# Projections as three one-pass float32r products, and attention masks read as int32 (one core)

## The reference, cut to what matters

```python
q = x @ Wq;  k = ctx @ Wk;  v = ctx @ Wv + bv      # float32, per layer
scores = where(mask == 0, -10000, q.k / 4)         # layer 0: int32 mask [8, 512, 512]
scores = where(causal, scores, -inf)               # layer 1: causal, no mask input
x = softmax(scores) @ v @ Wo + bo + x              # then normalisation and FFN
```

## Time and profile before

| | |
|---|---|
| median of 3 runs | 1360.01 us (1357.59 to 1364.4) |
| the profiled execution | 1357.38 us |
| its span | 1355.6 us |
| PE busy | 1256.7 us (93%) |
| DVE, ACT, POOL busy | 1001.9, 867.9, 512.4 us |
| mean DMA rate | 126 GB/s |

### The profile page before, as it was taken

One profiled execution on the slowest core, in us unless ns is written; L12 is line 12 of the kernel. 1 busy time (PEld: TensorE's weight loads), 2 busy tenths in 40 slices (PEclk: granted clock), 3 DMA queues, 4 the chain that ended last, 5 costly groups with the idle time before them and its releaser, 6 DMA issues. The chain is left out here.

```text
span 1355.6 us, 21435 instructions
## 1 busy us (share of the span) xinstructions
PE 1256.7 (93%) x7567; PEld 651.0 (48%) x7571; DVE 1001.9 (74%) x1724; ACT 867.9 (64%) x1483; POOL 512.4 (38%) x674
## 2 busy tenths in 40 slices
PE   9999799999999999999999999999998999980498
PEld 5566423334343433434555445545553785430298
DVE  5876588797878788786666688888773564996864
ACT  4455337676767777677665655565553666868693
POOL 4555300144343444435465433333333101656600
PEclk9999969999999999999999999999999999995699
DMA  8999684323334243433434553343101001326233
GB/s 288 379 344 323 237 178 114 101 65 101 97 105 131 64 130 80 114 95 102 122 84 110 150 173 94 103 120 101 60 18 48 1 0 47 140 93 232 78 109 109
DMA packets 88194, 170.82 MB, mean 126 GB/s; under 512 B 14866, under 2 KB 49430, under 8 KB 86550
## 3 DMA queue, kind: packets, MB, share of 16 engines
q1 hardware_dynamic: 87547, 168.16, 39.8%
q10 hardware_dynamic: 539, 1.26, 0.4%
HBM read 108.26 MB, written 60.31 MB: 124 GB/s over the span
## 5 line engine op out<-in xcount | busy, mean ns | idle before, releaser
L1341 DVE TENSOR_REDUCE b_neg_max<-b_score 128x1 f32<-128x512 f32 (+3 forms) x864 | 541.3, 663 | 177.6 <-PE b_score L886 93.5
L1111 ACT ACTIVATE b_probs<-b_exp 128x512 f32<-128x512 f32 (+1 forms) x864 | 463.2, 581 | 281.8 <-PE b_exp L910 281.1
L883 PE MATMUL b_score<-b_k_stack,b_q_stack 97*128 97x512 bf16 (+3 forms) x1024 | 356.0, 351 | 14.7 <-issue 8.8
L910 PE MATMUL b_exp<-b_q_stack,b_k_stack 100*128 100x512 bf16 (+3 forms) x1024 | 344.5, 341 | 6.4 <-ACT b_probs L1111 5.5
L931 PE MATMUL b_av<-b_probs,b_values 128*17 128x512 f32 (+3 forms) x2048 | 228.5, 518 | 3.7 <-POOL b_probs L1209 3.4
L883 PEld LDWEIGHTS b_score<-b_k_stack,b_q_stack 97*128 97x128 bf16 x1024 | 99.8, 98 | 250.5 <-DVE b_neg_max L1341 128.2
L910 PEld LDWEIGHTS b_exp<-b_q_stack,b_k_stack 100*128 100x128 bf16 x1024 | 100.1, 98 | 82.9 <-ACT b_probs L1111 24.9
L1209 POOL TENSOR_SCALAR_AFFINE_SELECT b_probs<-b_probs 128x512 f32<-128x512 f32 x96 | 61.7, 643 | 176.8 <-ACT b_probs L1111 176.2
L1217 POOL CAST b_max_parts<-b_neg_max 128x16 bf16<-128x16 f32 x64 | 12.9, 202 | 286.2 <-DVE b_neg_max L1341 283.9
L886 PE MATMUL b_score<-diag_qk,minus_big 128*128 128x128 bf16 x512 | 112.6, 220 | 0.0
L1625 PE MATMUL f_bank<-normed,f_w_upT 128*128 128x512 f32 x192 | 82.7, 592 | 0.0
(11 more groups left out here) (231 smaller groups left out, 2021.5 us busy)
## 6 DMA issues: line engine op xcount, KB each, us to landing
b_q_stack<-s_q SPq DMA_DIRECT2D x384, 64.0 KB
s_k<-a_part_k SPq DMA_DIRECT2D x48, 256.0 KB, 3.2
b_k_stack<-s_k SPq DMA_DIRECT2D x61, 192.0 KB
s_up<-f_up SPq DMA_DIRECT2D x6, 1536.0 KB, 5.1
s_va<-a_va SPq DMA_DIRECT2D x16, 544.0 KB, 5.5
b_values<-s_va SPq DMA_DIRECT2D x16, 544.0 KB, 4.4
a_mask_q<-mask_in SPq DMA_DIRECT2D x8, 1024.0 KB, 8.3
b_k_stack<-s_k SPq DMA_DIRECT2D x61, 128.0 KB
```

Of the source, the lines that this page charges most:

```text
L883: mm = pe.matmul(o, q, KS[half][0:R_MAX, h, 0:w], start=True, stop=causal or not general)
L910: mm = pe.matmul(o, k, QS[half][0:NSTACK, h, q0:T], start=True, stop=not masked)
L1111: nc.scalar.activation(probs[kc][:, h0:h0 + m, q0:T], exp_bank[n % RINGS][:, 0:m * w].rearrange("p (h n) -> p h n", h=m), ACT.Exp).then_in ...
L1341: nc.vector.tensor_reduce(neg_max[u][:, qt, h0:h0 + m], score_bank[n % RINGS][:, 0:m * w].rearrange("p (h n) -> p h n", h=m), AX.X, ALU.ma ...
```

## The change

Each float32 operand of the projections becomes a high half, rounded to float32r, and a low half, the remainder. A product becomes three one-pass products that add up in PSUM: low weight by high source, high by high, high by low.

- Weights, once: ACT and DVE split `wk0`; POOL splits `wv0`, `wk1`, `wv1`, `wq0` (a copy and a subtraction of 512 columns each) ahead of its first `split`.
- Context, per batch: ACT's `halve(b + 1)` (1,024 columns) comes after the copies of turned x; POOL's `ctx_remainder(b + 1)` (1,024 columns) comes between its two operations on `k1`. The low half lies where the context was. For batch 0 DVE makes it.
- Turned x: ACT copies both halves from PSUM, DVE subtracts both (it copied one). Both results have one buffer in place of two.
- Masks: only those of batches 0 and 1 are stored as bfloat16. For n = 2 to 7 attention loads the int32 mask in two halves of 512 KB, in slots t = 4(n - 1) and t + 1, and POOL turns each into bfloat16 in that same slot (`take_mask`, 1,024 columns), ahead of the next slot's `split`.
- Some semaphores of attention are merged, with the same order of work.

```diff
@@ project_phase, tensor
-                    for c in range(DC):
-                        mm = pe.matmul(o[:, :], w["w" + n][:, c, m * P:(m + 1) * P], src[:, c, :], ...)
+                    wh, wl = high["w" + n], low["w" + n]
+                    terms = [(wt, src, c) for wt, src in ((wl, src_high), (wh, src_high), (wh, src_low)) for c in range(DC)]
+                    for k, (wt, src, c) in enumerate(terms):
+                        mm = pe.matmul(o[:, :], wt[:, c, m * P:(m + 1) * P], src[:, c, :], ...)
...
-                pe.wait_ge(ctx_landed[half], 16 * (b // 2 + 1))
+                    pe.wait_ge(ctx_rest, b)
@@ project_phase, scalar
+            def halve(b):
+                act.wait_ge(ctx_landed[b % 2], 16 * (b // 2 + 1))
+                nc.scalar.activation(CT_high[b % 2][:, :, :], CT[b % 2][:, :, :], ACT.Copy).then_inc(ctx_halved, 1)
@@ project_phase, gpsimd
+            def ctx_remainder(b):
+                pool.wait_ge(ctx_halved, b + 2)
+                nc.gpsimd.tensor_tensor(CT_low[b % 2][:, :, :], CT[b % 2][:, :, :], CT_high[b % 2][:, :, :].bitcast(F32), ALU.subtract).then_inc(ctx_rest, 1)
...
+            for n, landed, count in SPLIT_BY_POOL:
+                pool.wait_ge(landed, count)
+                nc.gpsimd.tensor_copy(high[n][:, :, :], w[n][:, :, :]).then_inc(cut, 1)
+                pool.wait_ge(cut, split_of(n) - 1)
+                nc.gpsimd.tensor_tensor(low[n][:, :, :], w[n][:, :, :], high[n][:, :, :].bitcast(F32), ALU.subtract).then_inc(cut, 1)
@@ project_phase, vector
-                dve.wait_ge(x_turned, 2 * b + 2)
-                nc.vector.tensor_copy(XT[b % 2][:, 1, :], bank[(12 * b + 8) % 7][:, :]).then_inc(x_by_dve, 1)
+                for c in range(DC):
+                    dve.wait_ge(x_by_act, DC * b + c + 1)
+                    nc.vector.tensor_tensor(XT_low[:, c, :], bank[(12 * b + 7 + c) % 7][:, :], XT_high[:, c, :].bitcast(F32), ALU.subtract).then_inc(x_by_dve, 1)
@@ project_phase, sync
-                store_mask(b)
+                if b < STORED_MASKS:
+                    store_mask(b)
@@ attention_phase, sync
+            def fetch_mask_half(n, part):
+                sp.wait_ge(mask_cut, 2 * (n - STORED_MASKS) + part)
+                sp.dma_start(MQ[:, :, :], dram["mask"][n].rearrange("(t p) n -> p t n", p=P)[:, 2 * part:2 * part + 2, :]).then_inc(mask_in, 16)
...
-                    if n < NB:
-                        fetch_masks(n)
+                if t >= G and t % G < 2 and t // G + 1 < NB:
+                    fetch_mask_half(t // G + 1, t % G)
@@ attention_phase, gpsimd
+            def take_mask(t, n, part):
+                pool.wait_ge(mask_in, 16 * (2 * (n - STORED_MASKS) + part + 1))
+                pool.wait_ge(av_done, TT * (t - part))
+                nc.gpsimd.tensor_scalar(DQ[n % 2][:, 2 * part:2 * part + 2, :], MQ[:, :, :], 0.0, None, ALU.is_equal).then_inc(mask_cut, 1)
...
                 for kc in range(TT):
+                    if kc == 3 and t >= G and t % G < 2 and t // G + 1 < NB:
+                        take_mask(t, t // G + 1, t % G)
```

More of the change, by code:

```diff
@@ L88, in project_phase @@
         CT = two("a_ctxT", [P, DC, T], F32)
+        ctx_at = nc.sbuf_base - 2 * 4 * DC * T
+        CT_high = two("a_ctx_high", [P, DC, T], F32R)
+        CT_low = [nc.alloc_sbuf_tensor_at(f"a_ctx_low{i}", [P, DC, T], F32R, offset=ctx_at + 4 * DC * T * i) for i in range(2)]
+        high = {n: sb(f"a_{n}_high", [P, DC, D], F32R) for n in const["early_at"]}
+        low = {n: nc.alloc_sbuf_tensor_at(f"a_{n}_low", [P, DC, D], F32R, offset=at) for n, at in const["early_at"].items()}
         MQ = two("a_mask_q", [P, TT, T], I32)
@@ L124, in project_phase @@
         values_stored = [sem(f"a_values_stored{i}") for i in range(2)]
-        mask_stored = [sem(f"a_mask_stored{i}") for i in range(2)]
+        masks_stored = sem("a_masks_stored")
         N_REST = 10
@@ L327, in values @@
                     t = 2 * u + j
-                    for c in range(DC):
-                        mm = pe.matmul(o[:, j * D:(j + 1) * D], CT[b % 2][:, c, t * P:(t + 1) * P], w[f"wv{l}"][:, c, :], start=(c == 0), stop=(c == DC - 1))
+                    xh, xl, wh, wl = CT_high[b % 2], CT_low[b % 2], high[f"wv{l}"], low[f"wv{l}"]
+                    terms = [(x, wt, c) for x, wt in ((xh, wl), (xh, wh), (xl, wh)) for c in range(DC)]
+                    for k, (x, wt, c) in enumerate(terms):
+                        mm = pe.matmul(o[:, j * D:(j + 1) * D], x[:, c, t * P:(t + 1) * P], wt[:, c, :], start=(k == 0), stop=(k == len(terms) - 1))
                 mm.then_inc(v_made[l], 1)
@@ L336, in _ @@
                 half = b % 2
-                pe.wait_ge(ctx_landed[half], 16 * (b // 2 + 1))
                 if b == 0:
-                    pe.wait_ge(k0_landed, 32)
-                columns(b, "k0", CT[half])
+                    pe.wait_ge(small_made, 2)
+                else:
+                    pe.wait_ge(ctx_rest, b)
+                columns(b, "k0", CT_high[half], CT_low[half])
                 if b == 0:
-                    pe.wait_ge(v0_landed, 16)
+                    pe.wait_ge(cut, split_of("wv0"))
                 values(b, 0, 0)
@@ L345, in _ @@
                 if b == 0:
-                    pe.wait_ge(k1_landed, 16)
-                columns(b, "k1", CT[half])
+                    pe.wait_ge(cut, split_of("wk1"))
+                columns(b, "k1", CT_high[half], CT_low[half])
                 if b == 0:
-                    pe.wait_ge(one_landed, 48)
+                    pe.wait_ge(cut, split_of("wv1"))
                 values(b, 1, 0)
@@ L362, in _ @@
                 if b == 0:
[L363 to L366, removed]
+                    pe.wait_ge(cut, split_of("wq0"))
+                pe.wait_ge(x_by_dve, DC * (b + 1))
+                columns(b, "q0", XT_high, XT_low)
             pe.wait_ge(tail, 6)
@@ L646, in attention_phase @@
         values_landed = [sem(f"values_landed{i}") for i in range(2)]
-        masks_landed = [sem(f"masks_landed{i}") for i in range(2)]
+        masks_landed = sem("masks_landed")
+        mask_in, mask_cut = sem("mask_in"), sem("mask_cut")
         score_full, score_read = sem("score_full"), sem("score_read")
@@ L1197, in queries @@
                     pool.wait_ge(second_out, b + 1)
[L1198 removed]
+                    nc.gpsimd.tensor_tensor(part[:, 2, :, :], full, part[:, 1, :, :], ALU.subtract).then_inc(rest_out, 1)
             def cut(t, kc):
```

103 lines of the change are left out of this document (61 added, 42 removed).

## The result

The kernel after takes 1406.97 us (median of 4 runs, 1406.9 to 1408.52), the kernel before 1358.97 in 4 runs (1357.59 to 1364.4). The ratio is 1.0359, with a 95% interval of 1.0342 to 1.0377: slower by 48 us. The forecast was slower, 1393 us, 1368 to 1416. The profiled execution after took 1408.52 us, its span is 1406.8, and the mean granted clock over it fell from 0.966 to 0.942.

The account below looks back on a forecast made before the run. TensorE, without idle time in the projections and attention's layer 0, was taken as the bound. 1357.4 - 10 (projections) + 31 (mask waits) + 12 (clock) = 1390.4 us, with the median 2.6 above: 1393, range 1368 to 1416.

Parts of the forecast that it names:

- part 4: Attention: TensorE waits six times at the turned maxima for POOL's half masks, 5.1 us each, 31 us in all.
- the second halves: Attention, one slot later: loops of 15.0 to 16.0 us, hidden in a 16.57 us loop with 0.5 to 1.5 left.
- the sum of 18.1: Attention: loop from turned maxima through SP's queue, landing, cut and split to the next, 18.1 us against 12.97.
- part 5: Attention: after each of six waits the granted clock falls to 0.50, costing 2 us each, 12 us in all.
- the clock holds: Rival for attention: pauses of 5 us cost no clock, so 1381 us; chance 0.13.
- parts 1 to 3: Projections: faster TensorE products, the other engines in the way and a later start, together -10 us.
- The start: Projections: POOL's weight splits delay the second batch from 24.54 to 28.5 us, +4.0.
- the end of part 2: Projections: 16.3 us per batch taken; if POOL wins the port before DVE's thirds, turned x 2.1 us later, batch 18.4.
- the shared port eats the gain: Rival for the projections: POOL takes the port ahead of DVE's thirds each batch, 18.4 us or more, 1404; chance 0.17.
- both halves wait: Rival for attention: both halves wait, or landings take 7 us, 6 x 3 us more, 1411; chance 0.09.
- attention's upper one: Upper bound for attention: landing 7, cut 2.79, clock 4 us, 1 us per second half: 6 x 13.3 = +80.
- stage one's lower one: Lower bound for the projections: -18 us, with 15.6 us per batch and batch 1 gaining 3.

Follow-up runs that it names:

- experiments 1 to 3: New projections with all masks stored as before, 1358.51 us; projections as before with new masks, 1406.67; the changed kernel with half masks fetched one slot earlier, 1358.21.
- experiment 4: The changed kernel with 22 dummy matmuls on TensorE ahead of each of the six waits: 1398.91 us.
- Experiment 3: The changed kernel with each int32 half mask fetched one slot earlier, POOL's cut left in place: 1358.21 us.
- experiment 9: Half masks fetched a slot earlier, masks waiting only for their own buffer's store, plus POOL's k1 operation waiting for DVE's thirds of q0: 1352.62 us.
- experiment 7: The kernel with half masks fetched a slot earlier, with POOL's context remainder of batches 1 to 7 left out: 1362.12 us.
- experiment 10: The 1352.62 us kernel (POOL's k1 operation waits for DVE's thirds), with POOL's second k0 operation also waiting for DVE's normalization: 1350.84 us.

## Why the prediction was right, and where it was not

**The masks (part 4): right in kind and place, one term too small.** The six waits stand at the turned maxima, with the DMA in front, as worked out; the second halves wait for nothing (no wait of TensorE in those loops), and experiments 1 to 3 show that these loads alone make the loss. Forecast: 6 x 5.1 = 31 us. Measured: 32.9 by the six waits, 33.3 by the loops. The terms for slot 4, forecast and (measured): 1.7 (1.72), 7.5 (7.16), 5.7 (4.66), cut 1.9 (2.78), split 1.1 (1.03). The cut is as long as POOL's addition of 2.79 in the earlier trace rows, and not near its clip; taking the middle was 0.9 us short per mask. In slot 4 the shorter landing made up for that. In the other five batches the mask was there 4.76 to 6.07 us behind issues 7.15 to 8.32 after the maxima's, and their loops were 1.4 us longer than the first on average. The six together, 18.6 each, are 0.5 above the sum of 18.1: the cut's 0.9 too little and a landing taken a little too long. The second halves had less room than it looks: in experiment 4, where the slow clock didn't stretch these loops, four of the six have TensorE at its turned maxima within 0.6 us of the end of the split, one of them after waiting 0.68 us for it (four of its second halves also went out 1.0 to 1.2 us later than here).

**The clock (part 5): right in kind, a third too small.** Forecast 12 us, measured 15.7 in the second loops: 2.6 per wait and not 2.0. Experiment 4 shows 11.6 of it by taking most of the waits' idle time away. The rows behind the first wait give 3.6 us of work at 0.50 and 2 at 0.82, so 3.6 x 0.5 + 2 x 0.18 = 2.2 us, for a second loop that was 2.0 longer; the forecast's 2 was made for such a case. Behind the next waits, which are longer (5.28 to 6.8 us where the first is 4.36), the second loops are 2.4 to 3.0 longer, though not by the length of the wait: the longest has 2.4. Experiment 3, without waits, has 1.00 over 240 to 600. The rival "the clock holds" (1381) is excluded. The Trainium skill, "TensorE: Matmul & The Clock Gate", section "What's actually happening", names throttled as the default and activity as what releases it. Both runs agree with it: with most of the same waits filled by useless matmuls the second loops cost 11.6 us less. The clock was put at nothing in the first stage, and there too it fell, behind waits of 2.1 to 3 us: that is part of the next point.

**The projections (parts 1 to 3): the step that failed.** The forecast's term was -10 us; it was +1.9. By pieces:
- The start: +4.0 forecast, 28.67 - 24.54 = +4.1. The number is right with some luck. By the forecast POOL's chain held the second batch up, and that chain came out well (the context's remainder was done at 28.30, 28.5 forecast); but TensorE has no idle time ahead of 28.67, it had only just finished the first q0. Its own start was 4.9 us late (10.48 for 5.58, behind DVE's `a_ctx_low`), and the other kernels of this kind started between 8.2 and 9.3 and had their second k0 at 27.0 to 29.7.
- Batch 1: -1 forecast, 50.67 - 28.67 = 22.0 against 21.4 before, +0.6. TensorE waits 2.6 us for the mask's count and 1.2 for turned x in it, and the clock is at 0.66 over 10 us.
- Batches 2 to 6: 16.3 us each forecast, 142.89 - 50.67 = 92.2 us for five, 18.4 each. Before, 92.9. This is the missing gain: 10.7 us. It can be added up: five times TensorE's own 15.6 (batch 4 takes 16.8 with a wait of 1.22) are 78.0; its waits in these batches are 3.02, 2.13, 1.22, 2.12 and 2.12, together 10.6; and the clock's two dips (0.79 over 8 us each) take up to 3.4. That makes 92.0. So three lost races for the port are 6.4 us, the late normalization of batch 2 is 3.0, the context's remainder 1.2, and the slow clock, which the forecast had in attention alone, up to 3.4.
- Batch 7 up to the first scores: 29.97 against 32.14 before, -2.2. Here DVE's thirds took 1.29 us, and the 2.3 per batch did come.

What was wrong is the choice at the end of part 2: "if POOL wins the port at 9.9 in place of DVE's thirds, turned x is 2.1 us later and the batch takes 18.4". I had the case, and put it as a rival at 0.17 (1404), with the other one in the sum. In the trace POOL wins in three of batches 3 to 6 (pairs of thirds of 3.24, 1.28, 3.24 and 3.24 us), the batches last 17.9, 16.8, 19.2 and 18.1, and the one of 16.8 is the one whose thirds took 1.28. Its normalization wasn't cut open by POOL either (1.38 us for 3.24), so this trace alone can't tell the two apart; experiment 9 can, since it changes the thirds and leaves the normalization cut. The 19.2 has the slow clock behind its wait. Batch 2 (20.2) has the wait for both stores, 3.80 us on DVE, and then the normalization 3.0 us late. Experiment 9 turns the port around by one wait and has 4.4 us of the gain; experiment 7 shows that a lighter POOL doesn't settle the contest for DVE. The Trainium skill, "SBUF — State Buffer", section "Who interferes with whom", has the rule behind it: a DVE instruction with two inputs in SBUF contends with a GpSimd instruction that reads SBUF, and the port pair that they share is an exclusive lock. The runs agree (1.28 alone, 3.24 behind one POOL operation, 4.49 behind two), and experiment 10 comes to 16.9, near the 16.0 that I had worked out from it as the least.

**The sum.** 31 + 12 - 10 = 33 forecast; 33.3 + 15.7 + 1.9 = 50.9 in the profiled executions, of 51.2 (0.4 more is in the first loop of attention). So the forecast for the profiled execution, 1390.4, was 18.1 short of 1408.5: 11.9 in stage one, 3.7 in the clock, 2.3 in the waits. In the medians it is 14, since these lie 48 apart and the two profiled executions 51.1. The measured 1407 is near the rival "the shared port eats the gain" (1404), with the masks' waits as forecast; "both halves wait" (1411) is near in time and wrong in kind. Two of the forecast's bounds are added up wrong: attention's upper one is 5.1 + 1.3 + 0.9 + 4 + 1 = 12.3 per mask by its own terms and so +74, not +80, and stage one's lower one is 4 - 3 - 18 = -17, not -18. Neither carries the range.

## What to carry to other kernels

When a load moves into the slot of its consumer, ask which in-order engine takes it and what that engine owes the critical path next: here POOL's wait for 512 KB stood ahead of a 1 us split for which TensorE waited, and one slot of lead took the 48 us to nothing. When TensorE is made faster, see who holds each resource that the next engine needs at the new time: a race for a shared port that the path's engine loses eats the gain, and a wait that decides it for the engine on the path can give part of it back. A wait of TensorE can cost more than it lasts: behind each of the six of 4.4 to 6.8 us came 2.0 to 3.0 us of loss in the next loop, and of three waits of 2.1 us one was followed by a slow clock.

## What was not expected of the hardware

- POOL's comparison of 1,024 columns of int32 into bfloat16 took 2.78 us, as long as its float32 addition (2.79) and 2.7 times its clip (1.04).
- Less work on POOL didn't make the stage shorter: without the context's remainder (experiment 7) batches 1 to 6 took 114.9 us against 114.3 in all, since POOL then arrived first at the port each time, and the first scores came 4.8 us later.
- Behind a wait of 2.12 us that ended at 120.58 the granted clock was 0.50 in the stretch of 123 to 125 us, with the fall while TensorE was already busy again. Behind two other waits of the same length, in the same execution, it stayed at 1.00 (86 to 90 and 140 to 144 us).
